# Cross attention with the scores computed a second time, keys on the partitions, in a decoder layer

## What is computed

```
H, D = 16, 8                                   # heads, width of a head
q, k, v = split(layernorm(x) @ w_qkv.T)        # 128 tokens each
k = concatenate([context_k, k]); v = concatenate([context_v, v])    # 256 keys
attn = softmax(einsum('bhnd,bhmd->bhnm', q * D ** -0.5, k))
out = einsum('bhnm,bhmd->bhnd', attn, v)
x = x + out.reshape(B, N, 128) @ w_proj.T + b_proj
```

## Time and profile before

| | |
|---|---|
| median of 3 runs | 1204.8 us |
| profiled execution, its own time | 1205.34 us |
| its span, first to last instruction | 1203.6 us |
| TensorE matmuls busy | 1148.1 us, 95% |
| VectorE busy | 918.6 us, 76% |
| ScalarE busy | 845.3 us, 70% |
| GpSimd busy | 423.3 us, 35% |
| granted TensorE clock, mean | 0.989 of 2.4 GHz |

### The profile page before, as it was taken

One profiled execution on the slowest core, in us unless ns is written; L12 is line 12 of the kernel. 1 busy time (PEld: TensorE's weight loads), 2 busy tenths in 40 slices (PEclk: granted clock), 3 DMA queues, 4 the chain that ended last, 5 costly groups with the idle time before them and its releaser, 6 DMA issues.

```text
span 1203.6 us, 31280 instructions
## 1 busy us (share of the span) xinstructions
PE 1148.1 (95%) x11818; PEld 868.1 (72%) x11851; DVE 918.6 (76%) x2146; ACT 845.3 (70%) x2374; POOL 423.3 (35%) x732
## 2 busy tenths in 40 slices
PE   5999999999999998999999999999995999999997
PEld 4788888888888877777777777777773565656555
DVE  5766776677667776888888888888877788888887
ACT  2666666666666667888888888888893765565654
POOL 3444444444444451323333223233312532232222
PEclk9999999999999999999999999999997999999999
DMA  7000000000000000000000000000400000000000
GB/s 162 2 1 2 2 2 2 1 2 2 2 2 2 2 6 10 11 10 10 11 10 11 14 11 10 11 10 11 115 2 1 2 10 10 10 10 10 10 10 10
DMA packets 20663, 16.04 MB, mean 13 GB/s; under 512 B 7042, under 2 KB 18596, under 8 KB 20516
## 3 DMA queue, kind: packets, MB, share of 16 engines
q1 hardware_dynamic: 20176, 13.90, 4.4%
q10 hardware_dynamic: 340, 0.14, 0.1%
HBM read 11.94 MB, written 2.10 MB: 12 GB/s over the span
## 4 chain that ended last, share of the span: by engine, by line
PE 63%; issue 15%; ACT 10%; POOL 6%; DVE 5%; DMA 1%; SPq 0%; POOLq 0%; DVEq 0%
PE ps L956 49%; PE ps L1101 7%; ACT probs L573 6%; POOL h_lo L491 5%; PE ps L1007 5%; ACT probsT L564 3%; ACT k_hi L568 1%; DVE xT L657 1%; DMA wv<-in_L_attn_W_v 1%; PE ps L1134 1%; PE ps L1141 1%; PE ps L1129 1%; DVE nmax L640 0%; PE ps L964 0%; DVE rsum L647 0%
## 5 line engine op out<-in xcount | busy, mean ns | idle before, releaser
L573 ACT ACTIVATE probs<-ps,nmax 128x256 f32<-128x256 f32 x512 | 239.7, 480 | 9.6 <-DVE nmax L797 9.1
L797 DVE TENSOR_REDUCE nmax<-ps 128x2 f32<-128x512 f32 x256 | 176.2, 688 | 48.2 <-PE ps L956 44.9
L956 PE MATMUL ps<-probsT,vm 128*32 128x128 f32 x2048 | 161.5, 279 | 0.0
L520 ACT COPY probsT<-ps 128x512 f32<-128x512 f32 x128 | 75.1, 586 | 117.9 <-PE ps L1007 117.9
L564 ACT COPY probsT<-ps 128x512 f32<-128x512 f32 x224 | 132.1, 590 | 34.7 <-PE ps L1101 32.5
L1101 PE MATMUL ps<-ident,probs 128*128 128x128 f32 x1024 | 153.8, 273 | 1.2 <-ACT probs L573 1.1
L526 ACT ACTIVATE probs<-ps,nmax 128x128 f32<-128x128 f32 x512 | 143.2, 383 | 6.6 <-DVE nmax L640 6.5
L491 POOL TENSOR_TENSOR h_lo<-wk,h_hi 128x512 f16<-128x512 f32 x64 | 74.1, 1158 | 184.6 <-ACT h_hi L621 181.7
L387 POOL TENSOR_TENSOR probs<-probs,rinv 128x512 f32<-128x512 f32 x128 | 133.3, 1042 | 14.0 <-DVE rinv L650 14.0
L613 ACT ACTIVATE wq<-ps 128x512 f32<-128x512 f32 x128 | 76.6, 599 | 72.1 <-PE ps L956 72.1
L956 PEld LDWEIGHTS ps<-probsT,vm 128*32 128x32 f32 x2048 | 92.8, 109 | 42.7 <-issue 42.6
(11 more groups left out here) (192 smaller groups left out, 2772.9 us busy)
## 6 DMA issues: line engine op xcount, KB each, us to landing
ctx_row<-in_ctx SPq DMA_DIRECT2D x32, 128.0 KB, 2.0
out_x<-x_all SPq DMA_DIRECT2D x8, 256.0 KB, 2.3
kT<-in_L_ffn_down_proj_w SPq DMA_DIRECT2D x1, 1024.0 KB, 10.9
wq<-in_L_attn_W_q SPq DMA_DIRECT2D x1, 512.0 KB, 5.0
wk<-in_L_attn_W_k SPq DMA_DIRECT2D x1, 512.0 KB, 9.3
wv<-in_L_attn_W_v SPq DMA_DIRECT2D x1, 512.0 KB, 10.6
wo<-in_L_attn_W_o SPq DMA_DIRECT2D x2, 256.0 KB, 6.4
x_all<-in_x SPq DMA_DIRECT2D x1, 256.0 KB, 3.2
```

What stands on the lines that cost most here:

```text
L520: nc.scalar.copy(probsT[:, u, :], ps[6][:, :]).then_inc(sa_pT_taken, 1)
L573: last = nc.scalar.activation(probs[:, g % 4, i * KEYS2:(i + 1) * KEYS2], ps[SCORE_BANKS2[g]][:, i * KEYS2:(i + 1) * KEYS2], ACT.Exp, bias ...
L797: nc.vector.reduce_max(nmax[:, g, 0:2], ps[SCORE_BANKS2[g]][:, :].rearrange("p (h k) -> p h k", h=2), AX_X, negate=True).then_inc(ca_max, 1)
L956: return nc.tensor.matmul(o, l, r, start=start, stop=stop, **kw)
```

## The change

The change rewrites `cross_attention` on all engines. A round has `UNITS = 4` steps of four heads each instead of 8 steps of two.

- The scores are still computed with queries on the partitions (`ps<-kT,q_part`), but only for the maximum (`nmax2`). Each head occupies 32 rows of the array (three parts of 8 rows: value, value, remainder; and 8 rows for the shift), so a matmul uses 32 of the 128 rows, and consecutive matmuls use different rows and different banks. `qm` and its four masking instructions (L824) go.
- When all 16 maxima of a batch are there, they are split into two float16 numbers in `padded`, and TensorE adds them to the 8 spare rows of the queries by eight matmuls of 128 columns into bank 5; ScalarE copies the result to `q_shifted`. One round after the first scores, TensorE computes the scores a second time with the keys on the partitions (`transposed_scores`, `ps<-q_shifted,kT`, eight matmuls of 128 columns a step); the product contains the subtraction of the maximum.
- ScalarE computes the exponentials of whole banks straight into `probsT`, two activations of 512 columns a step, without a bias and without a sum. The transposes L1101 and the copies L564 and L802 go.
- The values `va` have a column of ones beside the 8 of a head, so that the matmul gives the sum too. Its result is copied (`z_aug`), transposed back by four transposes, divided on VectorE (`rinv2`, `zn`), transposed once more and projected.
- The normalisations into `xn2` and `xn3` move from VectorE to GpSimd. The stage has one more round at its end (`NB + 3` instead of `NB + 2`), since the steps of a batch are spread over more rounds.

The core of the diff:

```diff
-G2 = 8
+UNITS = 4
+ROWS = 32
+SHIFT = 16.0
...
+def unit_heads(u):
+    return [(t, l) for t in (2 * (u // 2), 2 * (u // 2) + 1) for l in (2 * (u % 2), 2 * (u % 2) + 1)]
...
             def cross_attention(b, parity, valid, steps):        # ScalarE
                 for g in steps:
...
+                    if g == 0 and valid(-1):
+                        n = b - 1
+                        act.wait_ge(ca_shift_in_bank, n + 1)
+                        nc.scalar.copy(q_shifted[:, n % 2, :, :], ps[5][:, :]).then_inc(ca_shifted, 1)
...
+                    if valid(-1):
+                        t = UNITS * (b - 1) + g
+                        act.wait_ge(ca_scores_T, t + 1)
+                        if t >= 2:
+                            act.wait_ge(ca_values_applied, t - 1)
+                        for a in range(2):
+                            last = nc.scalar.activation(probsT[:, 2 * (t % 2) + a, :], ps[2 + a][:, :], ACT.Exp)
                         last.then_inc(ca_exp, 1)
...
+                    if g == 0 and valid(-1):
+
+                        n = b - 1
+                        dve.wait_ge(ca_max, UNITS * n + UNITS)
+                        nc.vector.tensor_scalar(padded[:, :, :, 24], nmax2[:, n % 2, :, :], 1.0 / SHIFT, None,
+                                                ALU.mult).then_inc(ca_max_high, 1)
+                        dve.wait_ge(ca_max_high, n + 1)
+                        nc.vector.scalar_tensor_tensor(out=padded[:, :, :, 25], in0=nmax2[:, n % 2, :, :], scalar=1.0 / SHIFT,
+                                                       in1=padded[:, :, :, 24], op0=ALU.mult,
+                                                       op1=ALU.subtract).then_inc(ca_max_padded, 1)
...
+            def apply_values(n, u):
+                pe.wait_ge(ca_exp, UNITS * n + u + 1)
+                if u == 0:
+                    pe.wait_ge(ca_context_values, n + 1)
+                    pe.wait_ge(ca_v_taken, n + 1)
+                    if n > 0:
+                        pe.wait_ge(ca_z_taken, n)
+                buf = 2 * ((UNITS * n + u) % 2)
+                for t in (2 * (u // 2), 2 * (u // 2) + 1):
+                    for k in range(2):
+                        for a in range(2):
+                            l = 2 * (u % 2) + a
+                            last = mm(ps[4][ROWS * l:ROWS * l + ROWS, t * P:(t + 1) * P], va[:, n % 3, k, 4 * t + l, :],
+                                      probsT[:, buf + a, (2 * (t % 2) + k) * P:(2 * (t % 2) + k + 1) * P],
+                                      k == 0, k == 1)
+                last.then_inc(ca_values_applied, 1)
+
+            def transposed_scores(n, g):
+                t = UNITS * n + g
+                if g == 0:
+                    pe.wait_ge(ca_shifted, n + 1)
+                if t > 0:
+                    pe.wait_ge(ca_exp, t)
+                for t4 in (2 * (g // 2), 2 * (g // 2) + 1):
+                    for k in range(2):
+                        for a in range(2):
+                            l = 2 * (g % 2) + a
+                            r = slice(ROWS * l, ROWS * l + ROWS)
+                            at = (2 * (t4 % 2) + k) * P
+                            last = mm(ps[2 + a][:, at:at + P], kT2[r, n % 3, t4, k * P:(k + 1) * P],
+                                      q_shifted[r, n % 2, t4, :])
+                last.then_inc(ca_scores_T, 1)
...
                 for g in steps:                                   # TensorE
                     if valid(0):
                         if g == 0:
-                            pe.wait_ge(ca_packed, 3 * b + 3)
+                            pe.wait_ge(ca_keys_taken, b + 1)
+                            pe.wait_ge(ca_k_packed, b + 1)
+                        if g > 0 or valid(-1):
+                            pe.wait_ge(ca_max, UNITS * b + g)
+                        for i, (t, l) in enumerate(unit_heads(g)):
+                            r = slice(ROWS * l, ROWS * l + ROWS)
+                            last = mm(ps[i % 2][:, (i // 2) * KEYS2:(i // 2 + 1) * KEYS2], q_part[r, b % 2, t, :],
+                                      kT2[r, b % 3, t, :])
                         last.then_inc(ca_scores, 1)
...
+                    if g == 0 and valid(-2):
+                        apply_values(b - 2, UNITS - 1)
+                    if g == 0 and valid(-1):
+                        pe.wait_ge(ca_max_padded, b)
+                        if valid(0):
+                            pe.wait_ge(ca_k_packed, b + 1)
+                        for t in range(4):
+                            mm(ps[5][:, t * P:(t + 1) * P], padded[:, t, :, :].rearrange("p l c -> p (l c)"),
+                               ident_h[:, :], True, False)
+                            last = mm(ps[5][:, t * P:(t + 1) * P], ident_h[:, :], q_part[:, (b - 1) % 2, t, :],
+                                      False, True)
+                        last.then_inc(ca_shift_in_bank, 1)
...
-            run_batches(pe, 0, NB + 2, cross_attention, range(G2))
+            run_batches(pe, 0, NB + 3, cross_attention, range(UNITS))
```

More of the change, by code:

```diff
@@ new lines, in cross_attention @@
+                    if g == 1 and valid(1):
+                        n = b + 1
+                        act.wait_ge(ca_q_in_bank, n + 1)
+                        nc.scalar.copy(q_hi[:, :, :], ps[5][:, :]).then_inc(ca_q_high, 1)
+                    if g == 2 and valid(1):
+                        n = b + 1
+                        act.wait_ge(ca_k_in_bank, n + 1)
+                        nc.scalar.activation(k_hi[:, :, :], ps[5][:, :], ACT.Identity,
+                                             bias=k_bias[:, 0:1]).then_inc(ca_k_high, 1)
@@ L1134, in cross_attention @@
                         nc.tensor.transpose(ps[7][:, 2 * P:3 * P], xn3[:, :], ident[:, :]).then_inc(ff_xT_in_bank, 1)
-                    if g == 2 and valid(-1):
-                        pe.wait_ge(ca_inverse_wide, b)
+                    if g == 1 and valid(-2):
+                        pe.wait_ge(ca_z_taken, b - 1)
+                        if valid(1):
+                            pe.wait_ge(ca_keys_taken, n + 1)
+                        for t in range(4):
+                            last = nc.tensor.transpose(ps[6][:, t * P:(t + 1) * P], z_aug[:, t * P:(t + 1) * P], ident[:, :])
+                        last.then_inc(ca_zq_in_bank, 1)
@@ new lines, in cross_attention @@
+                    if g == 3 and valid(1):
+                        if valid(-2):
+                            pe.wait_ge(ca_normalised, b - 1)
+                        if not valid(0):
+                            pe.wait_ge(ca_keys_taken, 1)
+                        mm(ps[6 if valid(0) else 4][:, 0:P], xT2[:, :], wqkvT[:, 2, :]).then_inc(ca_v_in_bank, 1)
+                    if g > 0 and valid(-1):
+                        transposed_scores(b - 1, g)
+                        apply_values(b - 1, g - 1)
```

462 lines of the change are left out of this document (206 added, 256 removed).

## The result

| | before | after |
|---|---|---|
| median, us | 1204.79 (1204.49 to 1204.92, 4 runs) | 1158.26 (1157.57 to 1159.54, 4 runs) |
| span of the profiled execution, us | 1203.6 | 1156.2 |
| granted TensorE clock, mean | 0.989 | 0.981 |

The change makes the kernel faster: the ratio is 0.961, with a 95% interval of 0.960 to 0.9625, so 46.5 us less. The forecast was 35.8 us less, 1169, with a range of 1148 to 1201.

What follows compares the result with a forecast made beforehand. TensorE's written order was taken as the bound. The terms -2.9 - 2.4 + 29 x (12.8 - 14.14) + 8.4 = -35.8 us took 1205.3 to 1169.5, as a median 1169, with a range of 1148 to 1201.

Steps and rivals of the forecast that it cites:

- the forecast's main case: Full rounds follow the walk as given, 12.4 to 13.2 us each; 1157 to 1182 us in all, chance 0.60.
- its sign: Distance between two `ps<-ident_h,padded` groups, a full round's period, would be 12.4 to 13.2 us.
- the rival with hidden waits: Full rounds: `padded` and ScalarE's copy come earlier, a round is 11.7 to 12.3 us; 1137 to 1155, chance 0.09.
- What bounds the kernel before: Cross-attention's full rounds: TensorE's written order is the bound, busy 404 of 409 us, 14.14 us a round.
- The walk through one round: Full round from the output projection's weight load: 12.8 us, being 11.3 work, 1.35 two waits, 0.1 hand-offs.
- TensorE's own work: TensorE in a full round: 14.1 - 6.1 - 0.2 - 0.5 + 3.0 + 1.1, about 11.3 us.
- That the 32-row matmuls overlap: Scores and second scores: matmuls run side by side in pairs, 0.35 us a scores group, 0.39 a second-scores group.
- The rival without overlap: Scores and second scores: no overlap at all, or one kind without overlap plus dearer tiling steps; 1209 and more, chance 0.03.
- one kind alone: Scores or second scores don't overlap: 0.6 or 0.7 us a round more, about 1189, chance 0.15.
- the steps between tilings: TensorE's tiling switches, taken at 0.13 us; rival: 0.12 more each, a round 1.5 longer, 1216, chance 0.08.
- The clock: Granted TensorE clock expected at 1.00; rival: waits drop it to 1.2 GHz, some 20 us a round, 1378, chance 0.03.
- The end: Last rounds of the stage: 10.3, 9.0 and 9.8 us, 29.1 where 20.70 stood.

Runs made afterwards that it cites:

- relief for ScalarE: The kernel before with ScalarE's exponentials not summed along the row (sums set to 1): 1199.44 us, ratio 0.9955.
- the kernel with the filled gap: Changed kernel plus eight matmuls of 112 columns a round, behind the context's keys and ahead of the second scores: 1156.55 us, 0.960 of the kernel before.
- the last version: Changed kernel with `padded` filled early, `xn2`'s transpose and copy moved into the gap, back-transposes ahead of `xn3`'s transpose: 1137.71 us, 0.944 of the kernel before.
- the experiment on the order within a group: Changed kernel issuing all score and second-score matmuls of one 32-row group before the other's, instead of alternating: 1161.37 us, 0.963 of the kernel before.

## Why the prediction was right, and where its sizes were off

The direction and the mechanism came true, and the 1158 lie in the forecast's main case (1157 to 1182), but by a margin of one microsecond and with some luck. The round of 12.2 us is below the 12.4 to 13.2 that the forecast named as its sign; it lies in the 11.7 to 12.3 of the rival with hidden waits, though both waits are there. The rounds brought 16.8 us more than forecast and round 1 0.3; the end (3.3 longer) and round 0 (1.2 longer) took 4.5 of that back.

**What bounds the kernel before** was right. Eight matmuls more, 0.39 us a round in the changed kernel, lengthen the kernel before by 0.41 us a round, and relief for ScalarE gives back only TensorE's 5.4 us of waits.

**The walk through one round** had the mechanism right: two waits, at the places and for the releasers it named, no third, and TensorE's order elsewhere. From its zero, the weight load of the output projection (711.13 in the round shown):

| point of the walk | forecast | measured |
|---|---|---|
| shift starts, `padded` there | 2.3 | 2.3 |
| second scores of step 0 start | 3.8 | 3.6 |
| query projection starts | 4.54 | 3.97 |
| second scores of step 1 done | 6.5 | 5.9 |
| scores of step 2 done | 7.85 | 7.25 |
| second scores of step 2 done | 9.25 | 8.7 |
| second scores of step 3 done | 11.6 | 11.2 |
| next output projection | 12.75 | 12.2 |

The term that was mis-sized is the price of the second scores of step 0 and the scores of step 1 behind them. The walk added 0.39 and 0.35; the two took 0.35 together, and 0.54 where they were put on the same rows. So of the 0.39 that the walk had too much, 0.19 is the two kinds running at once. Another 0.10 is the groups' own price, 0.32 each where they stand alone, and the last 0.10 the step between two tilings, which isn't there when one such group follows another: 0.54 and not 0.64. With these 0.39 and the 0.18 by which the second scores of step 0 start early (the shift took 0.46 and not 0.56, the hand-offs were shorter), the walk is 0.57 ahead, and stays there but for small sums. Over 29 rounds the 0.58 by which the round is shorter is 16.8 us.

**TensorE's own work** was forecast at 11.3. From start to start of the groups, the round has gaps of 0.52 (712.93 to 713.45) and 0.62 (714.13 to 714.75), which leaves 11.1. Inside it, scores and second scores took 2.3 where 3.0 was said, shift and back-transposes 1.0 for 1.1, values 4.0 for 3.9, and the projections and small groups 3.8, where the sum by subtraction had left 3.4. (As printed, the forecast's terms add up to 11.4, or to 11.2 without the 0.17 us of waiting inside the 14.1; its 11.3 stands between them.) The forecast waits, 0.55 and 0.8, were 0.5 and 0.6.

**That the 32-row matmuls overlap** was inferred from one group of 64-row float32 records. The rival without overlap (0.03, with 0.15 for one kind alone) was priced at 1209 and more; with one group of rows for everything the kernel took 1213. So this inference carried the sign of the forecast. The other rivals fell: the waits were not hidden, the steps between tilings cost no more than taken (a group with its step is 0.32, under its price), and the clock stayed at 1.00 in the full rounds. "One kind doesn't overlap" is out by the same rows, 0.32 us for either kind.

**The clock**, forecast at 1.00, was not looked at where it did move. Round 0 took 9.7 where the chain said 8.5, and from 462.7 us on its clock was 0.50: its key projection takes 2.00 us to the next group (463.81 to 465.81), where it takes 1.10 in a full round (718.38 to 719.48), 0.9 of the 1.2 missing. It was 0.50 again among the last second scores (848.4 to 851.8) and in the stage's last microseconds.

**The end** was 3.3 us longer than forecast, by its three parts: 9.8 for 10.3, 10.8 for 9.0, 11.8 for 9.8. In the second part the stretch at the lower clock accounts for some 1.5 us (one group of values takes 1.86 instead of 1.00, 848.78 to 850.64, the next 1.30, and two groups of second scores 0.37 more between them). In the kernel with the filled gap, whose end is the same program, the clock stayed at 1.00 there, and the end took 31.2 and not 32.4. In the third the forecast had the back-transposes right behind the values; in the written order the transpose of `xn3` stands ahead of them and waits 2.10 us for GpSimd. In the last version, which swaps the two, this part is 1.6 us shorter. And GpSimd's normalisation, put at 0.1 more than before, costs 0.5 more each time: from the end of the statistics to the transpose it was 1.47 (911.15 to 912.62) and is 2.00 (862.80 to 864.80), because the instruction itself takes 0.80 us there and took 0.35 on VectorE (the kernel before, then the changed one):

```profile
912.22 0.35 DVE L839 TENSOR_SCALAR xn<-x_all,mv,rstd 128x128 f32<-128x128 f32 x1 [1.06 <-POOL rstd L452]
```

```profile
863.95 0.80 POOL L418 TENSOR_SCALAR xn<-x_all,mv,rstd 128x128 f32<-128x128 f32 x1
```

In the full rounds that is hidden, as forecast.

What stays open is the clock: why it falls in round 0 and not in the full rounds, with two waits each, and why it stays low there for 10 us in one kernel and for 14, 20 or 31 in others. It is only described here, and some 4 us between two of these kernels can be this alone (the experiment on the order within a group has 4.4 more in rounds 0 and 1).

## What to carry to other kernels

Read a round by the distance from group start to group start, and ask of each group which array rows it uses: matmuls on different rows overlap. Four matmuls of 256 columns cost 0.32 us on two sets of 32 rows and 0.54 on one, two such groups on four sets 0.35 at the one place where they stood next to each other, and with all of a group on one set of rows the change would have gained nothing. When a chain over other engines stands in TensorE's way once a round, move its first link up in its own engine's program (16 us here) or put other work of TensorE into the gap (eight matmuls were free there), and count that chain apart from the work. Check the last rounds by themselves: instructions that are ordered for full rounds wait there for other engines with nothing to cover the wait. And compare the stretches of lower clock before a few microseconds between two variants are given a cause.

## What the runs showed of the hardware

- Matmuls on different groups of 32 array rows run at once, and not only in the order of the program: a later one (scores, rows 64 to 127) starts at 714.78, ahead of six earlier ones (second scores, rows 0 to 63), which start from 714.82 on. The order inside a group changed the full rounds by 0.04 us, the choice of rows by 1.5. The Trainium skill (TensorE: Matmul & The Clock Gate, Part 3, What overlaps and what doesn't) says that matmuls start and end in program order; it also says that matmuls on different rows run at once, which agrees. By the start times of these rows the order doesn't hold across groups of rows, and the measurement decides. The ends in a trace are modelled and can't be used for it.
- A small float32 transpose beside another group on all 128 rows costs 0.07 us, and not the 0.16 between its start and the next group's (711.13 to 711.29): 711.12 to 711.61 with the output projection, 711.12 to 711.54 for that alone.
- The clock went to 0.50 behind waits of TensorE of 0.39, 1.13 and 0.30 us (ahead of 459.02, 460.87 and 462.65), and behind 0.51, 0.68 and 0.43 (845.4 to 848.3); two waits of 0.46 and 0.45 in a round of 12.2 us left it at 1.00 for 354 us. No rule follows from these: in the kernel with the filled gap waits of 0.50, 0.68 and 0.43 at the same place left it at 1.00, and with one group of rows it stayed at 0.50 from 485 to 490 us while TensorE was busy throughout.
